# A decoder layer with gathered experts: the gathered rows turned by a DMA transpose instead of by TensorE

## The chip, the cores and the metric

The kernel runs on one core of a Trainium2 chip. The metric is the device time of one execution, in microseconds (us). The kernel before took 889.33 us (median of 3 runs, 887.21 to 890.68).

## What is computed

A post-norm decoder layer on x of shape (8, 256, 256), so 2048 tokens of width D = 256: causal attention with 16 heads, then cross attention of the slot kind against a context of 120 rows with three rounds of a GRU cell, then a feed-forward part with a shared MLP and eight experts. After each of the three parts the result is added to x and normalized. The change lies in the experts:

```python
router_probs = softmax(x @ gate_w + gate_b)
expert_values, expert_indices = top_k(router_probs, k=2)      # normalized to a sum of 1
h = gelu(einsum('bsd,edi->bsei', x, ew1) + eb1)               # E = 8, D = 256, I = 1024
all_outputs = einsum('bsei,eid->bsed', h, ew2) + eb2
moe_out = sum over the two chosen experts of value * all_outputs
return x + shared_mlp(x) + moe_out
```

## The kernel before, in words

Every engine has its own program, and semaphores order them. Products are made in f16 with each f32 operand parted into a high and a low half; three of the four products are kept (high by high, high by low, low by high; `HILO`).

**The expert stage.** The 4096 choices (2048 tokens, two experts each) are sorted by expert into `NTILE` = 39 tiles of 128 rows, each of one expert. For tile i the following is done:

- GpSimd gathers 128 rows of x with two weights each from DRAM into `xg[i % 2]` by an indirect DMA (`gather`, issued at L1731). It waits for `picks` of tile i - 2, and for the transposes of tile i - 2.
- TensorE turns the tile: `turn(i)` (L1837) is two f32 transposes of 128x128 into PSUM bank 7, and it waits for `g_lo` and `g_hi` of the tile before, which say that the bank is read out.
- ScalarE copies the bank to f16, the high half (`turned`, L2310, counts `g_hi`); VectorE subtracts that from the bank, the low half (`turned`, L2354, counts `g_lo`), and then makes the row weights from the last two columns of `xg` (L2357 and L2359, they count `picks`). The halves are `xgT[i % 2]`, in two buffers.
- TensorE makes the hidden units, `up_chunk`: 8 chunks of 6 matmuls of 128 columns (L2219), and for another tile the output, `down_chunk`: 8 chunks of one matmul of 512 and one of 256 columns (L2227, L2228).
- The hidden units go PSUM to SBUF in two halves of 512 columns: VectorE adds the bias (`biased`, L2370, which waits for `U_mm` of the half), ScalarE applies the gelu (L2316) and then rounds all 1024 columns to f16 (L2322), VectorE makes the low half (`hidden_low`, L2375, counts `U_lo`).
- After the downs VectorE collects the output (`back`, L2386 and L2389), ScalarE weighs it (`weigh`, L2328), and GpSimd adds it to `back_y` in DRAM by an indirect DMA (`scatter`, L2191).

`tile_pair(up, ..., down, ...)` weaves the ups of tile i + 2 with the downs of tile i, so the expert stage is a row of such pairs, here called by the number of their ups: pair 2 to pair 38 have both parts or, for 0 and 1, ups alone. Ahead of the pair i + 2 stands turn(i + 3), so the turning is done one pair ahead of its use. A pair starts with waits for `g_lo` and `g_hi` of its ups, and for `U_lo` and `U_hi` of its downs.

The order on each engine is written out by hand. In round i of the loop they are, after the start-up:

```python
# TensorE : turn(i+3), [register load of 16 tile numbers when i+2 is a multiple of 16], tile_pair(i+2, i)
# ScalarE : turned(i+3), weigh(i-1), front(i+2)
# VectorE : turned(i+3), biased(i+2), back(i), hidden_low(i+2)
# GpSimd  : one gather, one scatter per tile
```

(`front` is the two gelus and the rounding.) So `turned(i+3)` on VectorE stands right behind `hidden_low(i+1)`, and on ScalarE behind `front(i+1)`.

**Around it.** The shared MLP runs ahead of the expert stage (L31 with `sw`) and its last eight chunks after pair 38. `ffn_sync` is SyncE's queue at the start of the stage: it stores the base values of `back_y` (`store_base`, L1745), waits for the first four gathers, stores another base and loads the expert biases `b2e` (L1777, 1 MB); after that, with `store_base(2)` in `experts_sync`, SyncE issues nothing until the last scatter. Then the rows are read back, normalized and stored.

Of the kernel before, what the change touches and what calls it, by code (L numbers as in the profile page):

```python
# [15 lines left out]
P = 128  # L16
# [18 lines left out]
def decoder_layer(nc, a, out):  # L35
# [23 lines left out]
    with top:  # L59
# [1581 lines left out]
        held.close()  # L1641


        with ExitStack() as c:
            e1 = sb(c, "e1", [P, E, DC, 2, I], F16)
            e2 = sb(c, "e2", [P, E, IC, 2, D], F16)
# [12 lines left out]
            he = [[part(xT_flat, 2 * I * (2 * u + i), I, F16).rearrange("p (k t) -> p k t", k=IC) for i in range(2)]  # L1659
                  for u in range(2)]  # L1660
            zf = part(slots_flat, 10 * I, I)
            xgT = [[part(slots_flat, 14 * I + 2 * D * (2 * u + i), D, F16).rearrange("p (c t) -> p c t", c=DC)
                    for i in range(2)] for u in range(2)]
            routes = sb(c, "routes", [P, 2 * I])
            route_at = itertools.count(0)

            def route(*shape):
# [44 lines left out]
            H_low = sem("H_low")  # L1712
            rows_in = [sem(f"rows_in{u}") for u in range(2)]
            rows_out = [sem(f"rows_out{u}") for u in range(2)]
            g_turned2, g_hi, g_lo = sem("g_turned2"), sem("g_hi"), sem("g_lo")
            U_mm, U_bias, U_gelu, U_hi, U_lo, D_mm, D_out = (
                sem(k) for k in ("U_mm", "U_bias", "U_gelu", "U_hi", "U_lo", "D_mm", "D_out"))
            gathered = [sem(f"gathered{q}") for q in range(NT // 2)]
# [15 lines left out]
            def store_tokens(g):  # L1734
                SY.wait_ge(n_norm, TG * (g + 1))
                SY.dma_start(rows_x[P + g * GT:P + (g + 1) * GT, 0:D].rearrange("(t p) d -> p t d", p=P),
                             xs[:, g * TG:(g + 1) * TG, :]).then_inc(x_stored, 16)

            BASES = (0, 1, NG - 1, 2)

# [14 lines left out]
            def ffn_sync():  # L1755
                SY.wait_ge(s_out, 2 * STEPS)
                for e in range(E):
                    for k in range(2):
                        if (e, k) in STORE_AT:
                            for g in STORE_AT[e, k]:  # L1760
                                store_tokens(g)
                        q = SHARED_PIECES + 4 * e + 2 * k
                        for p in (q, q + 1):
                            SY.wait_ge(p_out[p % STAGED], 16 * (p // STAGED + 1))
                        home = e1[:, e, :, :, :].rearrange("p c i n -> p c (i n)") if k == 0 else e2[
                            :, e, :, :, :].rearrange("p (h b) i n -> p h (b i n)", h=2)
                        SY.dma_start(home, halves[q:q + 2].rearrange("q p n -> p q n")).then_inc(e_in, 16)
                store_weights()
                for u in range(2):
                    SY.wait_ge(rows_in[u], 16)  # L1770
                for g in BASES[0:2]:
                    store_base(g)
                for u in range(2):
                    SY.wait_ge(rows_in[u], 32)
                store_base(NG - 1)
                SY.wait_ge(x_stored, 16 * NG)
                SY.dma_start(b2e, a["L0_ffn_eb2"].rearrange("(o e) d -> o e d", o=1).broadcast_to(  # L1777
                    (P, E, D))).then_inc(b2e_in, 16)
# [46 lines left out]
                    bass_reorder=False)  # L1825
                return list(values)

            def turn(i):

                PE.wait_ge(rows_in[i % 2], 16 * (i // 2 + 1))  # L1830
                if i == 0:
                    PE.wait_ge(count_mm, 2)
                if i >= 1:
                    PE.wait_ge(g_lo, i)
                    PE.wait_ge(g_hi, i)
                for ch in range(DC):
                    mm = PE.transpose(ps[:, 7, ch * P:ch * P + P], xg[:, i % 2, ch * P:ch * P + P], ident[:, :])  # L1837
                mm.then_inc(g_turned2, 1)

            def late_bank(m):  # L1840

                return m % IC % 2 + (6 if m >= MF else 0)
# [5 lines left out]
            def up(m):  # L1848
                g, k = m // IC, m % IC
                if m >= 2:  # L1850
                    PE.wait_ge(H_gelu, m - 1)
                if m == 0:
                    PE.wait_ge(sw_in, 16 * SHARED_PIECES)
                    PE.wait_ge(tr_out, 2 * STEPS)
                if m == 1:
                    PE.wait_ge(tz_out, 2 * STEPS)
                if m == MF:
                    PE.wait_ge(r_line, NAMED)
                if m == MF + 1:
                    PE.wait_ge(g_lo, NTILE)  # L1860
                    PE.wait_ge(g_hi, NTILE)
                if k == 0:
                    PE.wait_ge(n_lo, g + 1)
                    PE.wait_ge(n_hi, g + 1)
                w = [[s1c[i][:, ch, k * P:k * P + P] for i in range(2)] for ch in range(DC)]
                x = [[xT[:, g, i, ch, :] for i in range(2)] for ch in range(DC)]
                split_matmuls(PE, ps[:, late_bank(m), :], list(zip(w, x))).then_inc(H_mm, 1)
# [28 lines left out]
            def ffn_tensor():  # L1896
# [30 lines left out]
                for m in range(MF + 2):  # L1927
                    if m < MF:
                        up(m)
                    else:  # L1930
                        turn(m - MF)
# [244 lines left out]
            ffn_vector()  # L2176

            def experts_sync():
                store_base(2)

            def experts_pool():

# [13 lines left out]
                for i in range(2, NTILE + 6):  # L2196
                    if i < NTILE:
                        PO.wait_ge(picks, 2 * (i - 1))
                        PO.wait_ge(g_turned2, i - 1)
                        gather(i)  # L2200
                    if i >= 6:
                        scatter(i - 6)
# [9 lines left out]
            def experts_tensor():  # L2212
                def up_chunk(i, e, k):

                    u, q = i % 2, k // 4
                    w = [[e1[:, bass.ds(e, 1), ch, h, k * P:k * P + P].squeeze(1) for h in range(2)]
                         for ch in range(DC)]
                    for n, (ch, (h, j)) in enumerate(itertools.product(range(DC), HILO)):
                        yield PE.matmul(ps[:, 2 * u + q, (k % 4) * P:(k % 4) * P + P], w[ch][h], xgT[u][j][:, ch, :],  # L2219
                                        start=n == 0, stop=n == 3 * DC - 1)  # L2220

                def down_chunk(i, e, k):
# [8 lines left out]
                def tile_pair(up, e_up, down, e_down):  # L2231

                    if up is not None:
                        PE.wait_ge(g_lo, up + 1)
                        PE.wait_ge(g_hi, up + 1)
                    if down is not None:
                        PE.wait_ge(U_lo, down + 1)
                        PE.wait_ge(U_hi, down + 1)
# [47 lines left out]
                turn(2)  # L2286
                tile_pair(1, expert[1], None, None)
                for i in range(NTILE):
                    if i + 3 < NTILE:
                        turn(i + 3)  # L2290
                    if i + 2 < NTILE:
                        if (i + 2) % LOADED == 0:
                            expert += experts_from(mybir.EngineType.PE, i + 2)
# [9 lines left out]
                last_downs()  # L2303

            def experts_scalar():
                def turned(i):
                    SC.wait_ge(g_turned2, i + 1)
                    if i >= 2:
                        SC.wait_ge(U_mm, 2 * (i - 1))
                    SC.copy(xgT[i % 2][0], ps[:, 7, 0:D].rearrange("p (c t) -> p c t", c=DC)).then_inc(g_hi, 1)  # L2310

                def front(i):
                    for q in range(2):
# [13 lines left out]
                    SC.wait_ge(picks, 2 * (i + 1))  # L2327
                    SC.activation(yo[i % 2], yo[i % 2], ACT.Identity, scale=row_w[:, i:i + 1]).then_inc(weighed, 1)  # L2328

                turned(0)  # L2330
                turned(1)
                front(0)
                turned(2)
                front(1)
                for i in range(NTILE):
                    if i + 3 < NTILE:
                        turned(i + 3)
                    if i >= 1:
                        weigh(i - 1)
                    if i + 2 < NTILE:  # L2340
# [5 lines left out]
                    hidden(m)  # L2346

            def experts_vector():
                def turned(i):

                    VE.wait_ge(g_hi, i + 1)
                    if i >= 2:
                        VE.wait_ge(U_mm, 2 * (i - 1))
                    VE.tensor_tensor(xgT[i % 2][1], ps[:, 7, 0:D].rearrange("p (c t) -> p c t", c=DC), xgT[i % 2][0],  # L2354
                                     ALU.subtract).then_inc(g_lo, 1)
                    u, col = i % 2, slice(i, i + 1)
                    VE.tensor_tensor(picked[:, col], xg[:, u, D:D + 1], choice[0][:, col], ALU.mult).then_inc(picks, 1)  # L2357
# [33 lines left out]

                VE.wait_ge(r_line, TILES_KNOWN)
                expert = experts_from(mybir.EngineType.DVE, 0)
                turned(0)
                turned(1)
                shared_out(2)
                for i in range(2):
                    biased(i, expert[i])
                    hidden_low(i)
                    if i == 0:  # L2400
                        turned(2)
                        shared_base(2)
                for i in range(NTILE):
                    if (i + 2) % LOADED == 0 and i + 2 < NTILE:
                        expert += experts_from(mybir.EngineType.DVE, i + 2)
                    if i + 3 < NTILE:
                        turned(i + 3)
                    if i + 2 < NTILE:
                        biased(i + 2, expert[i + 2])
                    back(i, expert[i])  # L2410
# [127 lines left out]
```

## Time and profile before

| | us |
|---|---|
| median of 3 runs | 889.33 |
| lowest and highest | 887.21, 890.68 |
| the profiled execution's own time | 890.64 |
| its span in the trace | 889.4 |
| mean granted TensorE clock | 0.996 |

The profiled execution's own time is 1.2 us longer than its span and 1.3 us above the median. In all rows, times are us from the start of the span unless marked ns; PE is TensorE, PEld its weight loads, DVE is VectorE, ACT ScalarE, POOL GpSimd, SPq the DMA queue of SyncE. "L2219" is line 2219 of the kernel. Matmuls overlap in the rows: the distance from one start to the next start is what a matmul costs, not its duration.

### The profile page before, as it was taken

Reading aid. Unit: us, or ns where it says so; the run is one execution under the profiler, and the core shown is the slowest. Engines: PE = TensorE matmul, PEld = TensorE weight load, DVE = VectorE, ACT = ScalarE, POOL = GpSimd, SP = SyncE. Lnnn points to the kernel's source line nnn. Section 1 sums busy time; section 2 is a strip of 40 time slices with the busy share of each in tenths; the row PEclk is TensorE's granted clock in tenths of the full one; section 3 lists DMA queues with packets and bytes.
Section 4 is the critical chain, followed back from the end, with each engine's and each line's share of the span. In section 5 each row is a group of like instructions: output and inputs, shape, how many; then the busy total and the mean of one; then the engine's idle time right before and its main releaser. Section 6 shows DMA issues by size and latency. Waiting matters only on the chain. (4 is left out here: it accounts for less than half of the span.)

```text
span 889.4 us, 23089 instructions
## 1 busy us (share of the span) xinstructions
PE 859.9 (97%) x8094; PEld 680.0 (76%) x8094; DVE 606.1 (68%) x1669; ACT 557.2 (63%) x1251; POOL 377.8 (42%) x492
## 2 busy tenths in 40 slices
PE   5999999999999999999999999999999999999996
PEld 3888788888888888767676666676788888887864
DVE  3667588776667675756666667869677767766655
ACT  4988776777676776655756565564455555555555
POOL 1634354343433475324444332544534444444433
PEclk9999999999999999999999999999999999999999
DMA  9733424342424331410000000399423323333226
GB/s 317 207 126 113 142 97 152 119 160 96 143 94 138 103 119 49 62 42 2 1 1 1 2 1 1 105 393 356 158 52 50 49 44 50 49 50 50 43 27 195
DMA packets 61579, 88.04 MB, mean 99 GB/s; under 512 B 17279, under 2 KB 46527, under 8 KB 61343
## 3 DMA queue, kind: packets, MB, share of 16 engines
q1 hardware_dynamic: 53439, 75.52, 25.8%
q0 software_dynamic: 7488, 10.27, 7.3%
q8 instruction: 71, 1.16, 0.6%
q10 hardware_dynamic: 544, 0.79, 0.3%
q14 instruction: 37, 0.30, 0.1%
HBM read 56.00 MB, written 30.56 MB: 97 GB/s over the span
## 5 line engine op out<-in xcount | busy, mean ns | idle before, releaser
L648 POOL TENSOR_SCALAR prob<-prob,rden 128x128 f32<-128x128 f32 (+1 forms) x256 | 122.9, 498 | 183.1 <-DVE rden L949 183.0
L2219 PE MATMUL ps<-slots,e 128*128 128x128 f16 x1872 | 190.0, 219 | 2.2 <-DVE xs L2386 2.1
L2219 PEld LDWEIGHTS ps<-slots,e 128*128 x1872 | 152.6, 97 | 35.3 <-issue 4.4
L843 ACT ACTIVATE prob<-prob,nmx 128x128 f32<-128x128 f32 (+1 forms) x256 | 113.2, 444 | 29.8 <-DVE nmx L943 29.8
L2227 PE MATMUL ps<-e,xT 128*128 x312 | 117.3, 378 | 0.0
L2316 ACT ACTIVATE slots<-slots 128x512 f32<-128x512 f32 x78 | 49.1, 630 | 106.8 <-DVE slots L2370 106.8
L943 DVE CUSTOM_DVE_ANT_0 prob<-ps,mask 128x128 f32<-128x128 f32 (+1 forms) x256 | 73.7, 353 | 41.5 <-PE ps L730 41.5
L31 PE MATMUL ps<-xT,wqkv 128*128 128x256 f16 x768 | 97.2, 278 | 2.0 <-ACT slots L850 1.4
L31 PEld LDWEIGHTS ps<-xT,wqkv 128*128 128x128 f16 x768 | 73.4, 99 | 18.3 <-issue 6.9
L1731 POOL DMA_INDIRECT xg<-rows_x,dst x39 | 40.9, 1049 | 106.3 <-DVE mask L2359 103.0
L2228 PE MATMUL ps<-e,xT 128*128 x312 | 85.0, 273 | 0.0
L2375 DVE TENSOR_TENSOR xT<-slots,xT 128x1024 f16<-128x1024 f32 x39 | 47.8, 1225 | 39.9 <-ACT xT L2322 39.9
L2191 POOL DMA_INDIRECT back_y<-xs,dst x39 | 62.2, 1595 | 29.8 <-DMA back_y<-xs,dst 16.7
L2370 DVE SCALAR_TENSOR_TENSOR slots<-ps,b1e 128x512 f32<-128x512 f32 x78 | 53.7, 691 | 26.5 <-PE ps L2219 26.3
L592 DVE SCALAR_TENSOR_TENSOR parted<-piece,parted 128x256 f16<-128x256 f32 x144 | 59.8, 463 | 0.0
L31 PE MATMUL ps<-an,wqkv 120*128 120x256 f16 x432 | 58.9, 272 | 0.5 <-POOL an L1477 0.5
L730 PE MATMUL ps<-slots 64*128 64x128 f32 (+1 forms) x512 | 53.1, 345 | 2.5 <-ACT slots L850 2.5
L31 PEld LDWEIGHTS ps<-an,wqkv 120*128 120x128 f16 x432 | 41.2, 99 | 16.5 <-POOL an L1477 2.5
L31 PE MATMUL ps<-wst,whh 128*128 128x512 f16 x216 | 52.5, 379 | 0.0
L31 PE MATMUL ps<-s,whh 128*128 128x512 f16 x216 | 52.5, 379 | 0.0
L956 DVE COPY pT<-ps 128x768 f32<-128x768 f32 x32 | 30.6, 956 | 31.8 <-PE ps L700 31.8
L741 PEld LDWEIGHTS ps<-pT,v 128*64 128x64 f32 x768 | 42.4, 139 | 11.5 <-issue 11.5
(267 smaller groups left out, 1855.3 us busy)
## 6 DMA issues: line engine op xcount, KB each, us to landing
halves<-parted SPq DMA_DIRECT2D x36, 512.0 KB, 2.9
piece<-in_L_ffn_ew SPq DMA_DIRECT2D x32, 512.0 KB, 4.5
e<-halves SPq DMA_DIRECT2D x16, 1024.0 KB, 15.2
piece<-in_L_ffn_sh_w SPq DMA_DIRECT2D x4, 512.0 KB, 8.8
sw<-halves SPq DMA_DIRECT2D x4, 512.0 KB, 6.8
rows_x<-xs SPq DMA_DIRECT2D x4, 512.0 KB, 7.4
xs<-back_y SPq DMA_DIRECT2D x8, 256.0 KB, 4.4
out<-xs SPq DMA_DIRECT2D x8, 256.0 KB, 2.1
```

The source lines that it names most:

```text
L31: mm = pe.matmul(out, w, x, start=first and n == 0, stop=last and n == len(products) - 1, **kw)
L592: VE.scalar_tensor_tensor(share(piece_part(q, 1)), share(like_part(q)), WS, share(piece_part(q, 0)), ALU.mult, ALU.subtract).then_inc(p_lo, 1)
L648: PO.tensor_scalar(prob[u][:, h, r], prob[u][:, h, r], rden[u][:, h, t:t + 1], 1.0, ALU.mult, ALU.mult).then_inc(normed, 1)
L730: mm = PE.matmul(ps[:, 2 + 2 * p + h, query_tile(t)], qk[p][r, 0, t * P:t * P + P], qk[p][r, 1, 0:(t + 1) * P], start=True, stop=True)
L843: SC.activation(at, at, ACT.Exp, bias=nmx[u][:, h, t:t + 1], scale=-1.0, accum_out=den[u][:, h, t:t + 1]).then_inc(exped, 1)
L943: VE.tensor_tensor_reduce(prob[u][:, h, r], ps[:, 2 + h, r], mask[:, r], -SCALE, HIGHEST, ALU.add, ALU.min, nmx[u][:, h, t:t + 1]).then_in ...
L2191: PO.indirect_dma_start(back_y, bass.IndirectOffsetOnAxis(ap=dst[:, i:i + 1], axis=0), yo[i % 2], None, compute_op=ALU.add).then_inc(rows_ ...
L2219: yield PE.matmul(ps[:, 2 * u + q, (k % 4) * P:(k % 4) * P + P], w[ch][h], xgT[u][j][:, ch, :], start=n == 0, stop=n == 3 * DC - 1)
L2227: yield PE.matmul(ps[:, 4 + u, :], he[u][0][:, k, :], w, start=k == 0, stop=False, skip_group_check=True)
L2228: yield PE.matmul(ps[:, 4 + u, 0:D], he[u][1][:, k, :], w[:, 0:D], start=False, stop=k == IC - 1, skip_group_check=True)
L2316: SC.activation(z, z, ACT.Gelu_apprx_tanh).then_inc(U_gelu, 1)
L2370: VE.scalar_tensor_tensor(z, ps[:, 2 * u + q, :].rearrange("p (k t) -> p k t", k=4), 1 / WS, bias, ALU.mult, ALU.add).then_inc(U_bias, 1)
```

## The change

A gathered tile is no longer turned by TensorE. ScalarE rounds it to f16 in SBUF as it lies (`rows_high`), VectorE makes the low half beside it (`rows_low`), into `row_parts[i % 2]` of 128 x 512 f16, and SyncE issues one DMA transpose of all 512 columns into `xgT[i % 3]` (`turn_rows`). The transposed tile has three buffers, the parted rows have two. TensorE's `turn` goes away, with its wait; the ups wait for the DMA's semaphore (`rows_turned`); the gather waits for `picks` alone. In `ffn_sync` the first two `turn_rows` stand ahead of the base stores, and `turn_rows(2)` behind the load of `b2e`. In the start-up ScalarE now parts tile 2 ahead of `front(0)`, and VectorE does it ahead of `hidden_low(0)`.

```diff
+            row_parts = [part(routes, (3 + u) * I, 2 * D, F16) for u in range(2)]
+            xgT = [part(routes, (5 + u) * I, 2 * D, F16).rearrange("p (k t) -> p k t", t=P) for u in range(TURNED)]
...
+            def turn_rows(i):
+
+                SY.wait_ge(g_lo, i + 1)
+                if i >= TURNED:
+                    SY.wait_ge(U_mm, 2 * (i - TURNED + 1))
+                SY.dma_start_transpose(out=xgT[i % TURNED], in_=row_parts[i % 2]).then_inc(turned_in[i % TURNED], 16)
+
+            def rows_turned(engine, i):
+
+                engine.wait_ge(turned_in[i % TURNED], 16 * (i // TURNED + 1))
...
                 store_weights()
-                for u in range(2):
-                    SY.wait_ge(rows_in[u], 16)
+                turn_rows(0)
+                turn_rows(1)
                 for g in BASES[0:2]:
                     store_base(g)
...
-            def turn(i):
-
-                PE.wait_ge(rows_in[i % 2], 16 * (i // 2 + 1))
...
-                for ch in range(DC):
-                    mm = PE.transpose(ps[:, 7, ch * P:ch * P + P], xg[:, i % 2, ch * P:ch * P + P], ident[:, :])
-                mm.then_inc(g_turned2, 1)
...
             def experts_sync():
+                turn_rows(2)
                 store_base(2)
+                for i in range(TURNED, NTILE):
+                    turn_rows(i)
...
                         PO.wait_ge(picks, 2 * (i - 1))
-                        PO.wait_ge(g_turned2, i - 1)
                         gather(i)
...
                     if up is not None:
-                        PE.wait_ge(g_lo, up + 1)
-                        PE.wait_ge(g_hi, up + 1)
+                        rows_turned(PE, up)
...
                 for i in range(NTILE):
-                    if i + 3 < NTILE:
-                        turn(i + 3)
...
-                def turned(i):
-                    SC.wait_ge(g_turned2, i + 1)
+                def rows_high(i):
+                    SC.wait_ge(rows_in[i % 2], 16 * (i // 2 + 1))
+                    if i == 0:
+                        SC.wait_ge(r_line, TILES_KNOWN)
                     if i >= 2:
-                        SC.wait_ge(U_mm, 2 * (i - 1))
-                    SC.copy(xgT[i % 2][0], ps[:, 7, 0:D].rearrange("p (c t) -> p c t", c=DC)).then_inc(g_hi, 1)
+                        rows_turned(SC, i - 2)
+                    SC.copy(row_parts[i % 2][:, 0:D], xg[:, i % 2, 0:D]).then_inc(g_hi, 1)
...
-                turned(0)
-                turned(1)
+                for i in range(3):
+                    rows_high(i)
                 front(0)
-                turned(2)
                 front(1)
                 for i in range(NTILE):
                     if i + 3 < NTILE:
-                        turned(i + 3)
+                        rows_high(i + 3)
...
-                def turned(i):
+                def rows_low(i):
 
                     VE.wait_ge(g_hi, i + 1)
-                    if i >= 2:
-                        VE.wait_ge(U_mm, 2 * (i - 1))
-                    VE.tensor_tensor(xgT[i % 2][1], ps[:, 7, 0:D].rearrange("p (c t) -> p c t", c=DC), xgT[i % 2][0],
+                    VE.tensor_tensor(row_parts[i % 2][:, D:2 * D], xg[:, i % 2, 0:D], row_parts[i % 2][:, 0:D],
                                      ALU.subtract).then_inc(g_lo, 1)
...
                 for i in range(NTILE):
                     if (i + 2) % LOADED == 0 and i + 2 < NTILE:
                         expert += experts_from(mybir.EngineType.DVE, i + 2)
                     if i + 3 < NTILE:
-                        turned(i + 3)
+                        rows_low(i + 3)
```

## Rows read from the trace of the kernel before

**Rows 1.** The page, busy time of each engine: us, share of the span, instructions.

```profile
PE 859.9 (97%) x8094; PEld 680.0 (76%) x8094; DVE 606.1 (68%) x1669; ACT 557.2 (63%) x1251; POOL 377.8 (42%) x492
```

**Rows 2.** Windows: length, busy us by engine, granted clock, DMA share, GB/s.

```profile
0.00:10.00 10.00, 2.20 (x8) 1.42 (x8) 1.70 (x3) 4.00 (x5) 2.28 (x15) 1.00 0.76 258
...
642.00:848.00 206.00, 203.79 (x2376) 172.02 (x2376) 142.77 (x288) 107.57 (x180) 90.53 (x70) 1.00 0.30 52
```

**Rows 3.** Timeline of TensorE: the first matmuls of pair 2.

```profile
642.37 0.35 PE L2219 MATMUL ps<-slots,e 128*128 128x128 f16 x3
```

**Rows 4.** Timeline of TensorE: a border between two pairs, with the transposes.

```profile
756.05 0.27 PE L2228 MATMUL ps<-e,xT 128*128 x1
756.16 0.38 PE L1837 MATMUL ps<-ident,xg 128*128 128x128 f32 x2
756.46 0.35 PE L2219 MATMUL ps<-slots,e 128*128 128x128 f16 x3
756.69 0.38 PE L2227 MATMUL ps<-e,xT 128*128 x1
```

**Rows 5.** Timeline of TensorE: the border before pair 38, where no turn is left.

```profile
847.73 0.27 PE L2228 MATMUL ps<-e,xT 128*128 x1
848.00 0.35 PE L2219 MATMUL ps<-slots,e 128*128 128x128 f16 x3
848.24 0.38 PE L2227 MATMUL ps<-e,xT 128*128 x1
```

**Rows 6.** Timeline of VectorE around the same stretch: start, us, idle before it.

```profile
750.72 0.69 DVE L2370 SCALAR_TENSOR_TENSOR slots<-ps,b1e 128x512 f32<-128x512 f32 x1 [0.65 <-PE ps L2219]
...
753.19 1.22 DVE L2375 TENSOR_TENSOR xT<-slots,xT 128x1024 f16<-128x1024 f32 x1 [0.99 <-ACT xT L2322]
754.33 0.42 DVE L2354 TENSOR_TENSOR slots<-ps,slots 128x256 f16<-128x256 f32 x1
...
756.36 0.69 DVE L2370 SCALAR_TENSOR_TENSOR slots<-ps,b1e 128x512 f32<-128x512 f32 x1 [0.64 <-PE ps L2219]
```

**Rows 7.** Timeline of ScalarE in the same stretch.

```profile
751.45 0.63 ACT L2316 ACTIVATE slots<-slots 128x512 f32<-128x512 f32 x1 [0.71 <-DVE slots L2370]
752.11 1.04 ACT L2322 CAST xT<-slots 128x1024 f16<-128x1024 f32 x1
753.06 0.37 ACT L2310 CAST slots<-ps 128x256 f16<-128x256 f32 x1
```

**Rows 8.** Instruction groups of the turning: busy us, mean ns, idle before.

```profile
L1837 PE MATMUL ps<-ident,xg 128*128 128x128 f32 x78 | 15.0, 274 | 0.3 <-DMA xg<-rows_x,dst 0.3
```

**Rows 9.** DMA issues: queue, count, KB each, median us from issue to landing.

```profile
rows_x<-xs SPq DMA_DIRECT2D x4, 512.0 KB, 7.4
...
out<-xs SPq DMA_DIRECT2D x8, 256.0 KB, 2.1
...
xs<-in_L_ffn_eb SPq DMA_DIRECT2D x1, 1024.0 KB, 5.9
...
xg<-rows_x,dst POOLq DMA_INDIRECT x39, 2.8
back_y<-xs,dst POOLq DMA_INDIRECT x39, 3.8
...
back_y<-zrow SPq DMA_DIRECT2D x1, 128.0 KB, 2.4
```

**Rows 10.** Timeline of POOL: a gather, and what it had waited for.

```profile
755.34 0.98 POOL L1731 DMA_INDIRECT xg<-rows_x,dst  x1 [2.76 <-DVE mask L2359]
```

**Rows 11.** Timeline at the start of the expert stage, VectorE, TensorE and SyncE's queue.

```profile
631.82 0.42 DVE L2354 TENSOR_TENSOR slots<-ps,slots 128x256 f16<-128x256 f32 x1 [2.69 <-ACT slots L2310]
...
634.06 3.12 PE L2219 MATMUL ps<-slots,e 128*128 128x128 f16 x48
...
638.22 1.51 SPq L1777 DMA_DIRECT2D xs<-in_L_ffn_eb  x1
...
640.93 0.42 DVE L2354 TENSOR_TENSOR slots<-ps,slots 128x256 f16<-128x256 f32 x1
```

More of the change, by code:

```diff
@@ L1641, in decoder_layer @@
         held.close()
+        TURNED = 3
         with ExitStack() as c:
@@ L1661, in decoder_layer @@
             zf = part(slots_flat, 10 * I, I)
-            xgT = [[part(slots_flat, 14 * I + 2 * D * (2 * u + i), D, F16).rearrange("p (c t) -> p c t", c=DC)
-                    for i in range(2)] for u in range(2)]
             routes = sb(c, "routes", [P, 2 * I])
+            row_parts = [part(routes, (3 + u) * I, 2 * D, F16) for u in range(2)]
+            xgT = [part(routes, (5 + u) * I, 2 * D, F16).rearrange("p (k t) -> p k t", t=P) for u in range(TURNED)]
             route_at = itertools.count(0)
@@ L1714, in decoder_layer @@
             rows_out = [sem(f"rows_out{u}") for u in range(2)]
-            g_turned2, g_hi, g_lo = sem("g_turned2"), sem("g_hi"), sem("g_lo")
+            g_hi, g_lo = sem("g_hi"), sem("g_lo")
+            turned_in = [sem(f"turned_in{u}") for u in range(TURNED)]
             U_mm, U_bias, U_gelu, U_hi, U_lo, D_mm, D_out = (
@@ L1826, in experts_from @@
                 return list(values)
-            def turn(i):
-                PE.wait_ge(rows_in[i % 2], 16 * (i // 2 + 1))
[L1831 to L1835, printed above, removed]
-                for ch in range(DC):
-                    mm = PE.transpose(ps[:, 7, ch * P:ch * P + P], xg[:, i % 2, ch * P:ch * P + P], ident[:, :])
-                mm.then_inc(g_turned2, 1)
             def late_bank(m):
@@ L1859, in up @@
                 if m == MF + 1:
-                    PE.wait_ge(g_lo, NTILE)
-                    PE.wait_ge(g_hi, NTILE)
+                    PE.wait_ge(count_out, 1)
+                    PE.wait_ge(r_line, 20)
                 if k == 0:
@@ L1929, in ffn_tensor @@
                         up(m)
-                    else:
-                        turn(m - MF)
                     for work in beside.get(m, ()):
@@ L2218, in up_chunk @@
                     for n, (ch, (h, j)) in enumerate(itertools.product(range(DC), HILO)):
-                        yield PE.matmul(ps[:, 2 * u + q, (k % 4) * P:(k % 4) * P + P], w[ch][h], xgT[u][j][:, ch, :],
+                        yield PE.matmul(ps[:, 2 * u + q, (k % 4) * P:(k % 4) * P + P], w[ch][h], xgT[i % TURNED][:, j * DC + ch, :],
                                         start=n == 0, stop=n == 3 * DC - 1)
@@ L2285, in experts_tensor @@
                 tile_pair(0, expert[0], None, None)
-                turn(2)
                 tile_pair(1, expert[1], None, None)
                 for i in range(NTILE):
-                    if i + 3 < NTILE:
-                        turn(i + 3)
                     if i + 2 < NTILE:
@@ L2393, in experts_vector @@
                 expert = experts_from(mybir.EngineType.DVE, 0)
-                turned(0)
-                turned(1)
+                rows_low(0)
+                rows_low(1)
                 shared_out(2)
@@ L2398, in experts_vector @@
                     biased(i, expert[i])
+                    if i == 0:
+                        rows_low(2)
                     hidden_low(i)
                     if i == 0:
-                        turned(2)
                         shared_base(2)
```

## The prediction

> **What bounds the kernel now.** I read the page first: TensorE is busy for 97% of the span [rows 1], so at first sight anything taken off it is time won. The change touches one stage only, the pairs of the experts, so I cut that stretch out. From 642 to 848 us TensorE is busy for 203.8 of 206 us at a granted clock of 1.00, the 2.4 GHz level [rows 2]; VectorE (142.8), ScalarE (107.6) and GpSimd (90.5) have room. Pair 2 begins at 642.37 [rows 3] and pair 38 at 848.00 [rows 5]: 36 periods in 205.6 us, 5.71 each. TensorE bounds the stage by its throughput.
>
> The question is what a turn costs TensorE. The transposes are 78, of 274 ns [rows 8], but matmuls overlap, so I compare borders. With a turn, the last down matmul of a pair starts at 756.05 and the first down matmul of the next at 756.69: 0.64 us apart [rows 4]. Only one border has no turn, since tile 39 doesn't exist: 847.73 to 848.24, 0.51 us [rows 5]. So most of the border is not the transposes; a turn is worth about 0.13 us.
>
> The second question is how much time the tile has between being ready and being used. VectorE's second bias of pair n-2 starts at 750.72, right after that pair's ups. Then gelu (751.45), rounding (752.11), low half of the hidden units (753.19), and only then the low half of tile n, at 754.33, done at 754.75 [rows 6, 7]. Pair n starts at 756.46 [rows 4]. So from the ups of pair n-2 to `g_lo` of tile n pass 754.75 - 750.72 = 4.03 us, and the spare time is 1.7 us, or some 1.6 with the shorter border. Today nothing has to fit in there. Tomorrow the whole DMA transpose has to.
>
> **The change, part by part.**
>
> *Removed from TensorE:* 39 turns. The 36 in steady state give 36 x 0.13 = 4.7 us if TensorE still bounds the stage, and nothing if it waits. Three early ones are worth 0.4 us more at most.
>
> *ScalarE and VectorE:* the same two operations per tile, 128x256, now with SBUF as the source instead of PSUM: 0.37 and 0.42 us today [rows 6, 7]. No row shows these very forms; I bound a change by 0.1 us either way and take zero. They keep their places in the two hand-written orders, behind `front` and `hidden_low` of pair n-2, so the 4.03 us stay.
>
> *The gather* loses its wait for TensorE, but the row says that it waits for VectorE's weights [rows 10], so it starts no earlier. It has nearly two pairs to land and takes 2.8 us [rows 9]: nothing. `rows_high` also waits for the transpose of tile n-2, which pair n-2 needed before it began: nothing.
>
> *Added:* 39 DMA transposes of 128 KB from SyncE's queue. That queue is empty in the steady state, and its wait for a free `xgT` is for pair n-3, long done. What counts is the latency L, from VectorE's last write over SyncE's wake-up, issue and landing to TensorE's start. The trace has no transpose. Rows around it: 256 KB out of SBUF 2.1 us, 128 KB plain 2.4, the gather of 129 KB in 128 rows 2.8, the accumulating scatter of 128 KB 3.8, 512 KB in a busy stretch 7.4 [rows 9]. The lower end is 2.1, the upper 7.4. A transpose moves 128 KB in small pieces of rearranged data, beside a gather and a scatter that are issued about then; it is nearest to the scatter, a 128 KB transfer that does more than copy. I take L = 3.8. An L under 1.6 is excluded as far as any row goes.
>
> By the Trainium skill (VectorE: DVE Perf Modes, section The three transpose paths) a 128x128 bf16 block takes the DMA crossbar 1309 ns and TensorE 390: a rule against this change. As an estimate, four such blocks one after the other would be 5.2 us before any fixed cost, and the stage would then come out near 955 us. No row here shows it.
>
> *The new period.* A loop now closes over two pairs. The second biases of two neighbouring pairs stand 756.36 - 750.72 = 5.64 us apart [rows 6], so pair n-1 started at 756.46 - 5.64 = 750.82 [rows 4], and from a pair's start to its second bias it is 756.36 - 750.82 = 5.54 us; then 4.03 us to `g_lo` of the tile two further on; then L; then that pair starts. Two periods are 5.54 + 4.03 + L = 9.6 + L. TensorE's own two periods would be 2 x 5.54 = 11.1, so the loop takes over from L = 1.5. At L = 3.8 the period is 13.4 / 2 = 6.7. The stage is 36 x 6.7 = 241.2 us against 205.6: **+35.6 us**. TensorE gains nothing from the turns then, and the two register loads of some 1.1 us that stand between pairs today are swallowed by the new waits (which this count, against 205.6, includes).
>
> *The start.* `g_lo` of tile 0 comes at 632.24 and pair 0 starts at 634.06 [rows 11]; now it must wait until about 632.1 + 3.8 = 635.9, +1.8. Pairs 0 and 1 have ups alone. SyncE's third transpose stands behind the load of `b2e`, issued at 638.22 for 1.51 us and landing after 5.9, at 644.1 [rows 9, 11], in the same queue, and behind `g_lo` of tile 2 (today 641.35, now some 1 us earlier by VectorE's new order). So pair 2 starts around 644.8 instead of 642.4: **+2.4 us**, which includes the 1.8. The base stores move 1 to 2 us later; they are needed by ScalarE's rounding of tile 0 near 640: nothing.
>
> *The end.* After pair 38 starts, the rest is as before. The sum is 35.6 + 2.4 = +38.0. On the profiled execution: 890.6 + 38 = 928.6; on the median, which lies 1.3 lower, 889.3 + 38 = **927.3, say 927 us**.
>
> **The rivals.**
>
> *A. The transpose is a long wait, L 3.2 to 5.3 (forecast), 0.50.* 917 to 956 us.
>
> *B. It is as quick as a plain transfer, 0.22.* L 2.1 to 3.2. At 2.4, the row of the plain 128 KB, the period is 6.0, the stage 216: +10.4, with 2 for the start 902 us. At 2.1 it is 896. For it: every plain row of this size. Against: none of them turns anything. The Trainium skill (Advanced Engine Details and Errata, section X-Bar Transpose) says that transposing DMAs on this chip are as fast as regular ones, which is this case.
>
> *C. It is slow, 0.16.* L over 5.3: at 6.2 the period is 7.9, the stage 284: +79, with 5 for the start 973 us; at 7.4 it is 8.5 and 995. For it: four blocks moved one after the other. A form of it is that TensorE, idle for some fifth of the time, is granted the 1.2 GHz level. Against that: in the first 10 us TensorE is busy for 2.2 and the clock is 1.00 [rows 2].
>
> *D. The latency is hidden, 0.12: the other side.* The place is the start of each pair, the price is the spare 1.6 us, and L under 1.5 decides. Or the spare time is greater than I read, because VectorE and ScalarE, with free moments, shorten the 4.03 us. Then TensorE still bounds and wins the 4.7 + 0.4 us: 884 us, at best 0.6% less. With a little of the wait left it is no change. The rows are against it: no transfer lands in under 2.1.
>
> **How the numbers follow.** About 0.5% (4.4 us) is what a measurement can tell here. Faster by more: half of D, 0.06. Within: the other half, 0.06. Slower: 0.88. The likeliest case gives 927. The range starts at 894 us, just under B's low end, and leaves D out; upwards it goes to 973, L = 6.2, and leaves half of C out: together nearly 2 in 10.
>
> **What would show it.** In the trace after, the end of VectorE's low half of the tile (`g_lo`) to the first up matmul of its pair should be 3.8 us where it was 1.7, with TensorE's idle time put down to the DMA into `xgT`, 36 times, some 1.2 us each. The period of two pairs less 9.6 us is L, whatever it is. TensorE's busy share of the stage falls from 99% to about 82%. The steady granted clock stays 1.00. Pair 2 starts 2.4 us later. I am wrong if TensorE doesn't wait for `xgT` (D), if the transposes land in 2.4 or over 5.3 us (B, C: only the size), or if the waits come from somewhere else, such as ScalarE's new wait for the gather or the transpose two tiles back.

## The result and the profile after

The changed kernel takes 934.41 us (median of 4 runs, 932.39 to 935.06), the kernel before, beside it, 888.88: a ratio of 1.051 (95% interval 1.049 to 1.054), 45.5 us slower. The profiled execution took 932.39 us, its span is 931.1, 41.7 more than the span before.

The page after, busy time of each engine:

```profile
PE 858.8 (92%) x8016; PEld 672.1 (72%) x8016; DVE 607.9 (65%) x1669; ACT 558.9 (60%) x1251; POOL 379.0 (41%) x492
```

TensorE has 78 instructions less and 1.1 us less work, but its share of the span fell from 97% [rows 1] to 92%. The windows of the stage from pair 2 to pair 38, and of two single pairs, 2 and 6 (columns as in [rows 2]):

```profile
646.00:889.80 243.80, 206.25 (x2304) 167.24 (x2305) 140.66 (x284) 106.76 (x177) 89.46 (x69) 0.97 0.37 59
646.00:653.60 7.60, 7.59 (x64) 5.78 (x65) 0.69 (x1) 0.63 (x1) 0.95 (x1) 0.67 0.20 52
673.76:680.70 6.94, 6.94 (x64) 5.52 (x65) 2.54 (x5) 1.55 (x4) 2.58 (x2) 0.75 0.49 75
```

The stage takes 243.8 us instead of 205.6 [rows 3, 5], or 6.77 per pair instead of 5.71: +38.2. It starts at 646.0 instead of 642.4: +3.6. After pair 38 begins, 41.3 us remain, 41.4 before. That adds up to the 41.7.

The +3.6 hides a larger loss. What stands ahead of the stage, and the change doesn't touch, differs from one profiled execution to the next: the first gather is issued at 624.83 before and at 621.24 after (between 621.2 and 625.1 in all profiles of this document). Counted from there to the start of pair 2, the start-up takes 17.5 us before and 24.8 after: +7.2. With the stage that is +45.4, as much as the medians differ by; the profiled execution after is 2.0 us under its median, the one before 1.8 over. Who TensorE waited for in the stage (us in total, times, longest):

```profile
PE ps L2220 <- DMA routes<-routes: 41.9, 29, 5.6
```

`routes<-routes` is the transpose, from the parted rows to `xgT`. The longest, of 5.6 us, is the one that ends with pair 2, so 36.3 us lie inside the stage, 28 waits of 1.3 us on average. Before, this list held 2.1 us in all. One pair of starts shows the loop, VectorE first:

```profile
689.88 0.42 DVE L2350 TENSOR_TENSOR routes<-xg,routes 128x256 f16<-128x256 f32 x1
...
693.91 0.69 DVE L2366 SCALAR_TENSOR_TENSOR slots<-ps,b1e 128x512 f32<-128x512 f32 x1 [2.62 <-PE ps L2220]
...
697.52 0.42 DVE L2350 TENSOR_TENSOR routes<-xg,routes 128x256 f16<-128x256 f32 x1
```

and TensorE, the last down matmul of pair 8 and the starts of the pairs 8 and 9:

```profile
687.58 0.35 PE L2220 MATMUL ps<-routes,e 128*128 128x128 f16 x3 [1.34 <-DMA routes<-routes]
...
692.91 0.27 PE L2229 MATMUL ps<-e,xT 128*128 x1
694.64 0.44 PE L2220 MATMUL ps<-routes,e 128*128 128x128 f16 x3 [1.46 <-DMA routes<-routes]
```

L2350 is the low half of the tile. That of tile 9 is done at 690.30, and pair 9 begins at 694.64: L = 4.34 us. That of tile 10 can only follow pair 8, whose last down matmul starts at 692.91; it is done at 697.94, and pair 10 begins at 700.51: L = 2.57. The queue of SyncE, 36 transposes of the stage (ns, min/median/max of issuing one):

```profile
L1746 SPq DMA_TRANSPOSE routes<-routes x36: 1189/1190/1476, 645.6 to 886.5; - x36
```

Issuing alone is 1.19 us, where a plain copy of the same bytes is 0.46 (below). A wait here is the distance from a pair's last down matmul to the next pair's first up matmul, less the 0.11 us that it takes where nothing is waited for; 29 of the borders after pair 2 have one of over 0.35 us. Taking L for these 29 from such rows, its least value is 2.56 us, 13 lie at 2.56 to 2.58, the median is 3.36, the mean 3.30, the highest 4.61. One of them, at pair 32 (L = 4.04), has a register load between the pairs as well.

### The profile page after: what moved, and what is told of

Its sections match the earlier page's. It is cut to its first block and busy times, and to the rows that moved or that the text cites. A ratio compares the mean times of both kernels' runs of the same rounds, so it can differ in the third digit from the quotient of the medians.

```text
span 931.1 us, 22858 instructions
## 1 busy us (share of the span) xinstructions
PE 858.8 (92%) x8016; PEld 672.1 (72%) x8016; DVE 607.9 (65%) x1669; ACT 558.9 (60%) x1251; POOL 379.0 (41%) x492
## 3 DMA queue, kind: packets, MB, share of 16 engines
q8 instruction: 70, 1.15, 0.5%
## 5 line engine op out<-in xcount | busy, mean ns | idle before, releaser
L2220 PE MATMUL ps<-routes,e 128*128 128x128 f16 x1872 | 196.4, 223 | 44.8 <-DMA routes<-routes 41.9
L2220 PEld LDWEIGHTS ps<-routes,e 128*128 x1872 | 156.8, 99 | 85.9 <-issue 55.5
L2228 PE MATMUL ps<-e,xT 128*128 x312 | 120.3, 388 | 0.0
L2229 PE MATMUL ps<-e,xT 128*128 x312 | 86.7, 278 | 0.0
L31 PEld LDWEIGHTS ps<-an,wqkv 120*128 120x128 f16 x432 | 41.3, 99 | 16.5 <-POOL an L1477 2.6
L741 PE MATMUL ps<-pT,v 128*64 128x128 f32 x768 | 49.0, 277 | 0.8 <-ACT v L863 0.8
```

The costliest lines, as they stand in the source:

```text
L31: mm = pe.matmul(out, w, x, start=first and n == 0, stop=last and n == len(products) - 1, **kw)
L2228: yield PE.matmul(ps[:, 4 + u, :], he[u][0][:, k, :], w, start=k == 0, stop=False, skip_group_check=True)
L2229: yield PE.matmul(ps[:, 4 + u, 0:D], he[u][1][:, k, :], w[:, 0:D], start=False, stop=k == IC - 1, skip_group_check=True)
```

## The experiments

All are compared with the kernel before, run on the same chip; "period" is the mean from the start of pair 2 to that of pair 38, over 36.

**A plain copy in place of the transpose.**

```diff
-                SY.dma_start_transpose(out=xgT[i % TURNED], in_=row_parts[i % 2])...
+                SY.dma_start(xgT[i % TURNED].rearrange("p k t -> p (k t)"), row_parts[i % 2])...
```

> The DMA transpose becomes a plain DMA copy of the same 128 x 512 f16 from SBUF to SBUF, so the experts get rows that are not turned; everything else is the changed kernel. Theory 1 (the stage is a loop over two pairs, 9.6 us plus the latency L of the transpose): a plain copy is issued in 0.36 us instead of 1.19 and should land within L = 1.6 to 2.4, so the mean period of the pairs falls from 6.77 to between 5.6 and 6.0 us and the time to about 892 to 908 us. Theory 2 (any DMA between VectorE and TensorE costs the same here, the turning itself nothing): L stays at 2.6 or more and the time stays within 5 us of 934.

915.2 us, ratio 1.029 (1.026 to 1.033). The copy's issue:

```profile
L1746 SPq DMA_DIRECT2D routes<-routes x36: 464/465/471, 648.7 to 870.0; - x36
```

The stage takes 225.4 us, so the period is 6.26, above what I gave. L is 2.09 to 2.15 us at its least (9 of 22 waits) and reaches 4.10, or 4.24 at pair 16, where a register load stands between the pairs. So the least L is 0.5 us lower with a plain copy, and 19 of the 46 us go away; the other 27 us come with the plain copy too. Theory 2 fell, theory 1 was right in kind and low in size.

The longer issue is not what makes the transpose slower. Its first packet moves 1.20 us after VectorE's low half and the copy's 1.15, although one is issued for 1.19 us and the other for 0.46. The difference is in the moving: where nothing disturbs them, the last packet starts at 2.07 to 2.12 us for the transpose (544 packets) and at 1.66 to 1.69 for the copy (144 packets).

**Half the transpose.** Only the high half is turned; TensorE reads it twice, so the low half's products are replaced by repeated ones.

```diff
-                SY.dma_start_transpose(out=xgT[i % TURNED], in_=row_parts[i % 2])...
+                SY.dma_start_transpose(out=xgT[i % TURNED][:, 0:DC, :], in_=row_parts[i % 2][:, 0:D])...
-                        ... xgT[i % TURNED][:, j * DC + ch, :],
+                        ... xgT[i % TURNED][:, ch, :],
```

> The transpose moves only the 256 columns of the high half; the low half is not turned and the matmuls read the high half in its place, as many as before. If L consists of a cost per transposed piece (issue 1.19 us for 512 columns), the issue falls to about 0.6 us, L to about 1.8, and the time by 36 x 0.4 = 14 us or more, to about 915 us. If L is a fixed latency, the issue and the time stay as in the changed kernel (within 4 us of 934).

924.6 us (1.040, 1.036 to 1.044), between the two. The issue hardly changes, 1.17 us in the median. The least L is 2.44 instead of 2.56, with 288 packets, the last at 2.00. So the issue is nearly fixed, and half the size is worth 0.12 us of L at the least. By the loop that is 2 us of the 10 us gained. The late low halves of the next experiment, worth some 4 us, are absent here (35 of 35 at 4.33 to 4.37), and inside the stage no pair behind pair 2 runs at a lower clock, where three did.

**GpSimd's order swapped.**

```diff
                 for i in range(2, NTILE + 6):
+                    if i >= 6:
+                        scatter(i - 6)
                     if i < NTILE:
                         PO.wait_ge(picks, 2 * (i - 1))
                         gather(i)
-                    if i >= 6:
-                        scatter(i - 6)
```

> Only the order on GpSimd is changed: scatter(i - 6) ahead of gather(i) instead of behind it, so that the scatter's 1.6 us of issuing no longer lie 1.9 to 3.5 us behind the low half of the tile. Theory A (while GpSimd issues a scatter, in the later part of these 1.6 us, completions reach the waiting engines late: in the changed kernel pairs start either 2.57 us after the low half, or not before the scatter's issue ends, 3.6 us after it, and the second bias waits for the same moment): L is 2.6 for nearly all pairs, from the last down matmul to the low half it is 4.3 always, the mean period falls from 6.77 to about 6.2, and the time by 20 us to about 914. Theory B (the scatter's data moving on the same DMA engines hold the transpose back): the scatter's data now move during the transpose, so L grows and the time is the same or longer (934 to 945).

937.1 us (1.056, 1.052 to 1.059). Both theories had a half right. In the changed kernel, 13 of the 35 low halves (tiles 4 to 38) come 4.7 to 5.5 us after the last down matmul two pairs before, instead of 4.33 to 4.34: the second bias is late, as that at 693.91 above, which starts just as GpSimd's issue of a scatter ends (692.19 + 1.59 = 693.78). With the swap all 35 are at 4.33 to 4.36, so that delay is gone. But the scatter's data now move beside the transpose, and L is 3.0 us or more for all waits but the first (median 3.4). The sum is no gain: 2.6 us more, within the intervals.

**No scatters for tiles 0 to 35.**

```diff
-                    if i >= 6:
+                    if i >= 6 and i - 6 >= NTILE - 3:
                         scatter(i - 6)
```

with the waits on the missing scatters replaced (VectorE waits for `weighed` before it reuses `yo`).

> The scatters of the tiles 0 to 35 are left out (so their experts' outputs are missing); tiles 36 to 38 keep theirs. Both theories on the scatter: L is 2.6 for all pairs and the period about 6.1 to 6.2, the time about 934 - 36 x 0.6 = 912 us. If instead the spread of L has nothing to do with the scatter, it stays between 2.6 and 4.6 and the time stays near 934.

929.1 us (1.045, 1.042 to 1.048), period 6.60, where both theories on the scatter gave about 912 us. The late bias is gone here too (35 of 35 at 4.33 to 4.37), but L still runs from 2.56 to 4.64 (4.75 at the register load), median 3.6. The scatter is not what spreads L in the changed kernel.

**The gather held back until the transpose has landed.**

```diff
                         PO.wait_ge(picks, 2 * (i - 1))
+                        rows_turned(PO, i - 2)
                         gather(i)
```

> In the changed kernel, GpSimd waits for the transpose of the tile before it issues the next gather into the same rows, so that no gather moves data beside a transpose. Theory (the spread of L from 2.57 to 4.6 us comes from the gather, which is issued 0.6 us after the transpose and whose packets are mixed with it on the 16 DMA engines): L is 2.6 for nearly all pairs with a wait, and the mean period falls from 6.77 to about 6.3, the time by 15 us to about 919. Rival (the spread has another cause, since in the run without scatters it was there with the gathers at the same place): L spreads as before and the time stays within 4 us of 934.

935.1 us (1.053, 1.050 to 1.057), as the rival said, L from 2.56 to 5.14. The gather isn't it either. The DMA queues of the changed kernel show what goes with it. First the window from the low half of tile 8 to the start of pair 8 (L = 2.56), then that of tile 9 (L = 4.34); queue 1 is SyncE's, queue 8 brings instructions (queue 0, GpSimd's, is left out); packets, MB, share of the 16 engines:

```profile
q1 hardware_dynamic: 544, 0.13, 25.7%
```

```profile
q1 hardware_dynamic: 544, 0.13, 15.6%
q8 instruction: 1, 0.02, 1.7%
```

One packet of instructions, some 16 KB through one of the 16 DMA engines, is in the second window and not in the first. I looked at this window of all 29 waits. The 11 with such a packet have L = 3.6 to 4.6 us. In ten of them the last packet of the transpose comes 2.9 to 3.5 us after the low half; the eleventh is pair 32, where it comes at 2.15 and the register load stands between. Of the 18 without one, 13 have L = 2.56 to 2.58 and last packets at 2.1, and five have L = 3.2 to 3.6 (pairs 13, 22, 31, 37, 38).

Three of these five (13, 22, 31) hold a packet of a second instruction queue, of 8 KB, as here at pair 13:

```profile
q14 instruction: 1, 0.01, 1.1%
```

The other two are the last pairs, for which GpSimd has no gather left and issues the scatter earlier, so that its data move beside the transpose as in the swapped run. In the late windows only 2 to 43 of the transpose's 544 packets come later than 2.15 us after the low half, where 34 would be one engine's share.

The run without scatters sorts the same way: the 11 of its 22 waits that hold a packet of either instruction queue have L = 3.5 to 4.6 us, among them pairs 13, 22 and 31; of the 11 without one, nine have 2.56 to 2.60, and the other two stand at the register loads. With the plain copy, the ten waits that hold a packet have L = 2.4 to 4.1; of the twelve without one, nine have 2.09 to 2.15 and one 2.31, and two stand at the register loads. With the gather held back the count is less clean: the ten waits with a 16 KB packet have L = 3.4 to 5.1, but of the 18 without a packet only seven are under 2.7 us.

So a DMA engine that is busy with an instruction packet seems to hold back its sixteenth of the transpose. No kernel was made that takes the instruction packets away; this is a count and not an experiment. It doesn't cover the whole delay: at pairs 22 and 31 the last packet is only 0.2 us late, and TensorE starts 1.2 to 1.3 us after it instead of 0.5.

**The parting one pair ahead.** The same work, but each tile is parted, and so its transpose issued, one pair earlier.

```diff
                 front(0)
+                rows_high(3)
                 front(1)
                 for i in range(NTILE):
-                    if i + 3 < NTILE:
-                        rows_high(i + 3)
+                    if i + 4 < NTILE:
+                        rows_high(i + 4)
...
                         shared_base(2)
+                        rows_low(3)
...
-                    if i + 3 < NTILE:
-                        rows_low(i + 3)
+                    if i + 4 < NTILE:
+                        rows_low(i + 4)
```

> The same work, but ScalarE and VectorE part tile n one pair earlier (tile i + 4 instead of i + 3 in round i), so that the transpose has a whole pair more to land. Theory 1: the spare time is then 1.6 + 5.5 us, more than any L seen (up to 4.6), TensorE waits for no transpose after the start, and the period is that of a pair without turns, 5.5 us: 36 x (6.77 - 5.52) = 45 us less than the changed kernel, about 889 us, equal to the kernel before within its start-up (+4). Rival (the transposes and gathers slow the stage by their load on the DMA engines or by GpSimd and not by their latency): the period stays above 6 us and the time above 908.

889.5 us, ratio 1.000 (0.999 to 1.001), 45 us less than the changed kernel. TensorE's waits in the stage, and the stage:

```profile
PE ps L2220 <- DMA routes<-routes: 4.1, 1, 4.1
PE ps L2220 <- DVE xs L2386: 3.2, 2, 1.7
```

```profile
648.46:848.81 200.35, 197.12 (x2304) 164.29 (x2305) 140.57 (x282) 106.69 (x177) 92.52 (x68) 0.99 0.45 71
```

The transposes and gathers are all still there, with a greater share of the DMA engines (0.45 against 0.37), and TensorE waits for one of them, at the start. So the loss of the steady state was latency in a place with no room for it, not load. The period is 5.57 us, 0.14 less than before the change; two second biases of VectorE in mid-stage:

```profile
754.71 0.69 DVE L2367 SCALAR_TENSOR_TENSOR slots<-ps,b1e 128x512 f32<-128x512 f32 x1 [0.44 <-PE ps L2220]
...
760.16 0.69 DVE L2367 SCALAR_TENSOR_TENSOR slots<-ps,b1e 128x512 f32<-128x512 f32 x1 [0.44 <-PE ps L2220]
```

5.45 us apart where it was 5.64 [rows 6]: 0.19 us per pair without turns.

**The third transpose ahead of the bias load.**

```diff
+                turn_rows(2)
                 SY.wait_ge(x_stored, 16 * NG)
                 SY.dma_start(b2e, ...
...
             def experts_sync():
-                turn_rows(2)
                 store_base(2)
```

> Only the place of the third transpose is changed: ahead of the load of the 1 MB of expert biases on SyncE's queue, instead of behind it. Theory (the transpose of tile 2, issued at 637.22, landed at 646.0 because it stood behind that load; TensorE waited 5.6 us and then ran at a granted clock of 0.68 for a pair, which was 2.3 us longer): pair 2 starts at 640.5 to 641.5, at full clock, and the time falls by 5 to 7 us, to about 928. Rival (it is the transpose's own latency or a shortage of DMA engines during the base stores): pair 2 starts after 645 as before and the time stays within 2 us.

929.6 us (1.044, 1.042 to 1.047), 5 us less than the changed kernel. The third transpose behind the load, in the changed kernel:

```profile
634.91 0.82 SPq L1790 DMA_DIRECT2D xs<-in_L_ffn_eb  x1
637.22 1.39 SPq L1746 DMA_TRANSPOSE routes<-routes  x1
```

and the start of pair 2 there, then, in this run, of pairs 2 and 3:

```profile
646.01 0.50 PE L2220 MATMUL ps<-routes,e 128*128 128x128 f16 x3 [5.61 <-DMA routes<-routes]
```

```profile
643.61 0.35 PE L2220 MATMUL ps<-routes,e 128*128 128x128 f16 x3 [1.26 <-DMA routes<-routes]
652.70 0.50 PE L2220 MATMUL ps<-routes,e 128*128 128x128 f16 x3 [3.48 <-DMA routes<-routes]
```

The order of the queue it was; the wait of 5.6 us falls to 1.3, and pair 2 runs at full clock. Its start at 643.6 is later than the 640.5 to 641.5 that I gave, but the first gather came 1.9 us later in this execution too: from the low half of tile 2 to pair 2 it is 3.8 us, where it was 8.8. The load now delays the fourth transpose, so part of it comes back at pair 3, which waits for 3.5 us and then runs at a clock of 0.77.

**Both edits,** and then with the order of the queue mended further. First both:

> Both of the last two edits. Theory: start-up like the kernel before, period 5.5: about 883 to 886 us, faster than the kernel before by some 4 us, because TensorE no longer turns and waits for nothing. Rival (a turn costs TensorE nothing that isn't hidden in the border between pairs, or 0.27 us each as its rows say): the same as before within 1 us, or 10 us less.

887.7 us (0.999, 0.997 to 1.001): 2 to 5 us above the 883 to 886 that I gave, with a wait of 2.9 us before pair 3 and a clock of 0.76 in it. It can't be told from the kernel before. Then two places for the load of the biases (`TURNED` is 3):

```diff
 # e_best_x: the load right behind the first two base stores
                 for g in BASES[0:2]:
                     store_base(g)
+                SY.wait_ge(x_stored, 16 * NG)
+                SY.dma_start(b2e, ...
...
                 store_base(NG - 1)
+                turn_rows(2)
...
             def experts_sync():
+                turn_rows(TURNED)
                 store_base(2)
 # e_best_y: the load behind the fourth transpose
                 store_base(NG - 1)
+                turn_rows(2)
+                turn_rows(3)
                 SY.wait_ge(x_stored, 16 * NG)
                 SY.dma_start(b2e, ...
```

> The parting one pair ahead, with the start put in order: the load of the expert biases right behind the first two base stores, then the third transpose, the fourth ahead of the last base store. In the run with the two edits before, pair 2 started at 641.68, but pair 3 waited 2.9 us and then ran at a granted clock of 0.76, 1.6 us longer. Theory: both go away, about 4.5 us less than that run: 883 us, and faster than the kernel before by some 6 us (0.6%). Rival (what is gained at pair 3 is lost where the earlier load holds back the gathers of tiles 2 and 3): 887 to 889.

891.9 us (1.004, 1.002 to 1.005), slower than the kernel before and than either theory gave. The third transpose is issued at 639.41, but in the queue it stands behind the load, which was issued at 634.45 and lands at 645.6, and behind a base store; pair 2 starts at 649.3. The rival was right in its direction and not in its reason: the gather of tile 3 landed 3.1 us after its issue, as without the early load (3.3 in the next run).

> As the run before it, but the load of the expert biases stands behind the fourth transpose: the transposes of tiles 2 and 3 come first, and the biases land after pair 2 has ended, so that VectorE's first output waits for them some 2 us. If that wait is covered by the spare time one pair ahead: 883 us. If not, 885 to 887.

886.6 us, ratio 0.9973 (0.9959 to 0.9987), in the second of the ranges that I gave: 2.3 us less than the kernel before, the one version faster than both, by little. Its stage takes 200.9 us at a clock of 1.00, 4.8 less than before; from the first gather to pair 2 it takes 19.5 us, 1.9 more than before. That leaves a gain of 2.9, near the 2.3 measured.

**Three turns per tile on TensorE,** in the kernel before.

```diff
-                for ch in range(DC):
+                for ch in (*range(DC),) * 3:
                     mm = PE.transpose(...)
```

> The kernel before, with each tile turned three times over by TensorE: 6 transposes instead of 2, same result. It measures what a transpose costs TensorE. If it is the 0.05 to 0.11 us between two starts, 39 x 4 x 0.06 to 0.11 = 9 to 17 us more than before: 898 to 906. If each cost its 274 ns, 43 us more: 932.

899.6 us (1.012, 1.010 to 1.014), inside the 898 to 906 that I gave: 10.6 us for 156 more transposes, 0.068 us each. The border with six of them:

```profile
757.69 0.27 PE L2228 MATMUL ps<-e,xT 128*128 x1
757.80 0.82 PE L1837 MATMUL ps<-ident,xg 128*128 128x128 f32 x6
758.45 0.33 PE L2219 MATMUL ps<-slots,e 128*128 128x128 f16 x3
```

From the last down matmul to the first up matmul it is 0.76 us, where it was 0.41 with two [rows 4]: 0.35 for four, 0.09 each. The rows' 274 ns are durations of overlapping instructions and no price.

## Why the prediction was right

It said 927 us in 894 to 973, slower with 0.88; 934 was measured. Step by step:

- **The reading of the spare time** (4.03 us to `g_lo`, some 1.6 us to spare, nothing there that could cover a DMA) is what the whole result hangs on. The run with the parting one pair ahead shows it for the stage: same operations, 45 us less.
- **The closed loop over two pairs** held: in most pairs the low half comes 4.33 to 4.34 us after the last down matmul two pairs before, as in the kernel before (32 of 35). In 13 of 35 it came up to 1.1 us later, by 9 us in all, which I had not foreseen; halved by the loop it is some 4 us of the stage.
- **L = 3.8** was too large. The least is 2.56, the mean of the 29 waits 3.3. With the loop this gives a period of (9.6 + 3.3) / 2 = 6.45, not 6.7.
- **The clock** was to stay at 1.00. The stage's mean is 0.97. The pairs 6, 15 and 33, after waits of 2.3 to 2.5 us, ran at 0.75 and took 6.8 to 6.9 us from first to last matmul instead of 5.3; pair 2, after 5.6 us, ran at 0.67 and took 7.6. Together 7 us, of which I had none in the sum, only as a form of rival C. So two terms that I left out, some 11 us, stand in for the 9 us by which my L was too large (36 x 0.25): the period came out at 6.77 against 6.70 by luck in the sizes.
- **The start** is the term that was furthest off. Pair 2 starts 3.6 us later than before instead of 2.4, but in an execution whose first gather was issued 3.6 us earlier; counted from that gather the loss is 7.2 us. The mechanism is the one named, the third transpose behind the bias load: moving it ahead of the load took the wait before pair 2 from 5.6 to 1.3 us. Most of the 7 us by which 927 fell short of the measured 934 are the 4.8 us missed here and the 2.6 us of the stage (38.2 against 35.6).
- **The turns:** I priced them at 0.13 us a pair from a single border without one. Three turns per tile give 2 x 0.068 = 0.14, but the pairs of the run one pair ahead follow each other 0.19 us closer, so something of the border itself goes too. A hidden transpose would thus gain 5 to 7 us in the stage; the best version gained 4.8 there and kept 2.3 of them.
- **The gather, the queue in the steady state, `rows_high`'s waits, the end:** nothing, as said. The operations from SBUF: 0.40 us on ScalarE instead of 0.37, 0.42 on VectorE as before.
- **The signs:** TensorE waited for the transpose 28 times inside the stage, and not 36, for 1.3 us on average; its busy share of the stage fell to 85%, where I gave 82.
- **Rivals A and B:** the mean L of 3.30 lies at the low edge of the forecast (3.2 to 5.3), and the 13 undisturbed waits, at 2.56 to 2.58, lie in rival B's range (2.1 to 3.2). The price of B was too low: even the plain copy in that place costs 27 us, not 7 to 13, because its L too is above the least in 13 of 22 waits, and because pair 2 starts later. The Trainium skill's statement (Advanced Engine Details and Errata, X-Bar Transpose) that transposing DMAs are as fast as regular ones doesn't hold for the latency of one of 128 KB: 2.56 against 2.09 us at the least, with packets that move for 0.9 us instead of 0.5. The estimate from its figure for a 128x128 block (VectorE: DVE Perf Modes, The three transpose paths), four blocks one after the other, 5.2 us, was too high.
- **Rival D** was excluded as argued: L was never under 2.56.

## What to carry to other kernels

An operation moved from a saturated engine to a DMA is free only where the data are ready a DMA's latency before they are used, so measure that time first (here 1.6 us, against the 2.1 us that even the plain copy took), and if it is missing, move the producer one round ahead in the hand-written order as part of the change. A latency that closes a loop over two rounds costs half of its excess per round, and the work taken off the engine is worth the distance between starts, not the duration in its row. When two profiled executions are compared, count from an event in front of the change, since what runs ahead of it may differ by some us. At the start of a stage, look at what large load stands ahead of the small urgent transfer in the same queue.

## What the runs showed that I had not expected

- Issuing a DMA transpose from SyncE takes 1.19 us for 512 columns and 1.17 for 256; a plain copy 0.46. Yet the first packet moves 1.20 us after the data are ready for both transposes and 1.15 for the copy.
- L is 1 us or more above its least value when an instruction packet of 16 KB moves in the same window (11 of 29 waits, one of them at a register load; none under 3.6 us), and 1.0 us above when one of 8 KB does (3 waits).
- TensorE's granted clock fell to 0.75 for the pair after a wait of 2.3 to 2.5 us in three of five cases (pairs 6, 15, 33; not after 2.27 us before pair 21 and 2.54 before pair 27), and to 0.67 after 5.6 us. These are means of the pair, between the two levels of 2.4 and 1.2 GHz. Each of the three waits cost 1.5 to 1.6 us more than itself. In the run with the third transpose ahead of the load it fell to 0.75 after a wait of 2.1 us too. Why one wait lowers it and another of the same length doesn't stays open.
- While GpSimd issues an accumulating scatter behind its gather, VectorE's second bias came up to 1.1 us late in 13 of 35 pairs (in 13 too with the third transpose ahead of the load, in 4 with the gather held back), and in none of them when the order was swapped, when the scatters were left out, when the transpose was a plain copy, or when it was half as wide. Why the transpose has a part in this stays open.
